# Keeping attention values unsplit in DRAM and splitting the first key block inside the head-pair loop

## What is computed

```
x = x + 0.5 * ffn(layernorm(x))      # routed low-rank experts, top 16 of 64
x = x + attn(layernorm(x))
x = x + 0.5 * ffn(layernorm(x))

# attn: 32 heads, the key and value width is 128
q, k, v = split(hidden @ wq), split(hidden @ wkv)
scores  = q @ k^T * scale, causal mask
attn    = softmax(scores) @ v
return attn.reshape(B, S, 32 * 128) @ wo
```

## Time and profile before

| | |
|---|---|
| median of 3 runs | 1045.79 us (1045.55 to 1046.63) |
| the profiled execution's own time | 1047.01 us |
| its span, first to last instruction | 1045.2 us |
| mean granted TensorE clock | 0.995 |
| TensorE busy | 1031.7 us, 99% of the span |
| VectorE, ScalarE, GpSimd busy | 689.6, 555.1 and 532.5 us |
| moved by transfers | 168.17 MB |

### The profile page before, as it was taken

One profiled execution on the slowest core, in us unless ns is written; L12 is line 12 of the kernel. 1 busy time (PEld: TensorE's weight loads), 2 busy tenths in 40 slices (PEclk: granted clock), 3 DMA queues, 4 the chain that ended last, 5 costly groups with the idle time before them and its releaser, 6 DMA issues.

```text
span 1045.2 us, 18708 instructions
## 1 busy us (share of the span) xinstructions
PE 1031.7 (99%) x5588; PEld 892.5 (85%) x5588; DVE 689.6 (66%) x1815; ACT 555.1 (53%) x1480; POOL 532.5 (51%) x472
## 2 busy tenths in 40 slices
PE   8999999999999999999999999999989999999998
PEld 8999788888788888888888888888878888889997
DVE  6778852433467677777667767766777988766553
ACT  4112455554366676676676676676676555531110
POOL 5431378996268777778777778777410000010000
PEclk9999999999999999999999999999989999999999
DMA  9700254772634443453443443443577878840000
GB/s 373 306 0 1 81 211 174 277 265 91 231 92 134 161 139 114 147 161 132 155 143 114 148 161 130 151 150 121 161 258 279 313 251 280 289 161 11 20 20 31
DMA packets 83704, 168.17 MB, mean 161 GB/s; under 512 B 8528, under 2 KB 24912, under 8 KB 82640
## 3 DMA queue, kind: packets, MB, share of 16 engines
q1 hardware_dynamic: 83664, 167.68, 46.5%
HBM read 102.37 MB, written 63.44 MB: 159 GB/s over the span
## 4 chain that ended last, share of the span: by engine, by line
PE 96%; DVE 2%; ACT 1%; DMA 1%; issue 0%; POOL 0%; POOLq 0%; ACTq 0%
PE bank L274 28%; PE bank L276 28%; PE bank L275 28%; PE bank L540 4%; PE bank L558 3%; PE bank L529 3%; PE bank L330 1%; PE bank L282 1%; DMA o_raw<-keep_o 1%; PE bank L356 0%; PE bank L517 0%; DVE x L1039 0%; DMA x<-x_in 0%; DVE ow_lo L935 0%; DVE o_lo L935 0%
## 5 line engine op out<-in xcount | busy, mean ns | idle before, releaser
L1280 POOL TENSOR_SCALAR ve<-mv 128x1 f32<-128x1 f32 x24 | 6.3, 264 | 309.3 <-DVE mv L942 309.1
L652 ACT ACTIVATE bank<-bank,nmax 128x128 f32<-128x128 f32 (+1 forms) x256 | 105.7, 455 | 1.2 <-DVE nmax L1056 1.1
L1069 DVE TENSOR_SCALAR prob<-bank,rinv 128x128 f32<-128x128 f32 (+1 forms) x256 | 95.1, 413 | 4.6
L1056 DVE CUSTOM_DVE_ANT_0 bank<-bank,mask 128x128 f32<-128x128 f32 (+1 forms) x256 | 83.6, 389 | 18.7 <-PE bank L276 18.7
L274 PE MATMUL bank<-xc_lo,wq_hi 128*128 128x512 f32 x224 | 93.4, 417 | 1.0 <-ACT s7q L606 0.7
L274 PE MATMUL bank<-o_lo,ow_hi 128*128 128x512 f32 x224 | 89.7, 401 | 4.0 <-DVE o_lo L935 4.0
L276 PE MATMUL bank<-o_hi,ow_hi 128*128 128x512 f32 x224 | 88.4, 395 | 0.0
L275 PE MATMUL bank<-o_hi,ow_lo 128*128 128x512 f32 x224 | 88.2, 394 | 0.0
L274 PE MATMUL bank<-xc_lo,wk_hi 128*128 128x512 f32 x224 | 87.6, 391 | 0.3 <-ACT s L606 0.3
L276 PE MATMUL bank<-xc_hi,wq_hi 128*128 128x512 f32 x224 | 87.8, 392 | 0.0
L606 ACT CAST o_hi<-o_raw 128x1024 fp32r<-128x1024 f32 x56 | 59.2, 1057 | 53.4 <-DMA o_raw<-keep_o 44.6
(11 more groups left out here) (166 smaller groups left out, 3153.4 us busy)
## 6 DMA issues: line engine op xcount, KB each, us to landing
o_raw<-keep_o SPq DMA_DIRECT2D x49, 512.0 KB, 4.1
keep_v<-out_hl SPq DMA_DIRECT2D x64, 256.0 KB, 2.3
v<-keep_v SPq DMA_DIRECT2D x64, 256.0 KB, 3.5
keep_o<-att_comb SPq DMA_DIRECT2D x60, 256.0 KB, 2.6
keep_o<-att SPq DMA_DIRECT2D x45, 256.0 KB, 3.2
stage_v<-wv SPq DMA_DIRECT2D x4, 2048.0 KB, 9.1
stage_wq<-wqk SPq DMA_DIRECT2D x16, 512.0 KB, 3.3
keep_vraw<-out_raw SPq DMA_DIRECT2D x64, 128.0 KB, 2.1
```

The source lines that it names most:

```text
L652: nc.scalar.activation(sp[b][:, a:e], sp[b][:, a:e], ACT.Exp, bias=nmax[:, c:c + 1], scale=-1.0, accum_out=rsum[:, c:c + 1]).then_inc(s["e ...
L1056: nc.vector.tensor_tensor_reduce(out=sp[b][:, a:e], in0=sp[b][:, a:e], in1=mask[:, a:e], scale=-SCALE, scalar=BIG, op0=ALU.add, op1=ALU.mi ...
L1069: nc.vector.tensor_scalar(prob[:, b, a:e], sp[b][:, a:e], rinv[:, c:c + 1], None, ALU.mult).then_inc(s["p_ready"], 1)
```

## The change

For every tile of V the plain sum is stored, even c too. The tiles out_hl and out_raw become one tile out_v for each of two buffers, `keep_v` and `keep_vraw` become one tensor, and the 32 lo subtractions and 24 of the 32 roundings of the V phase go (the other eight become plain copies of block 3). In the pair loop `load_v` puts the plain first key block where lo will stand (v_in is the same memory as v). ACT rounds it into the hi part (`act_v_split`), and DVE subtracts in place (`dve_v_split`), one instruction each for both sequences of a half, 128 partitions by 2x256 elements. Half 1 of pair p is split in stage 1 of pair p, half 0 of pair p + 1 in stage 3 of pair p, half 0 of pair 0 in the prologue: 32 instructions on each engine. TensorE now waits for the semaphore v_split where it waited for v0_loaded and v1_loaded. The core of the diff:

```diff
-                if c % 2 == 0:
-                    pe.wait_ge(s["v_low"], low_count(g - 1, 3, c))
-                else:
-                    pe.wait_ge(s["v_raw12"], 2 * (g - 1) + c // 2 + 1)
+                pe.wait_ge(s["v_raw12"], TH * (g - 1) + c + 1)
...
             if j == 0:
-                pe.wait_ge(s["v0_loaded"], 64 * p + 64)
+                pe.wait_ge(s["v_split"], 2 * p + 1)
             elif j == 2:
-                pe.wait_ge(s["v1_loaded"], 64 * p + 64)
+                pe.wait_ge(s["v_split"], 2 * p + 2)
...
         def act_v_last_block(act, g):
-            act_v_high(act, g, 3, 0)
-            act_v_plain(act, g, 1)
-            act_v_high(act, g, 3, 2)
-            act_v_plain(act, g, 3)
+            for c in range(TH):
+                act_v_plain(act, g, c)
+
+
+        def act_v_split(act, p, half):
+            act.wait_ge(s[f"v{half}_loaded"], 64 * p + 64)
+            act_copy(v[:, half, :, 0, :], v_in[:, half, :, 1, :]).then_inc(s["v_hi_done"], 1)
...
                 act_attended(act, p, j)
+                if j == 1:
+                    act_v_split(act, p, 1)
+                elif j == 3 and not final:
+                    act_v_split(act, p + 1, 0)
...
-        def dve_v_low(dve, g, block, c):
-            dve.wait_ge(s["v_hi_done"], low_count(g, block, c))
-            lo(out_high(block, c, 1), v_src(block, c), out_high(block, c, 0)).then_inc(s["v_low"], 1)
+            wait_stored(dve, g, block, c)
+            nc.vector.tensor_tensor(out_plain(block, c), a, b, ALU.add).then_inc(s["v_sum"], 1)
+
+        def dve_v_split(dve, p, half):
+            dve.wait_ge(s["v_hi_done"], 2 * p + half + 1)
+            lo(v[:, half, :, 1, :], v_in[:, half, :, 1, :], v[:, half, :, 0, :]).then_inc(s["v_split"], 1)
...
                 if j < 2 or not final:
                     dve_softmax_max(dve, u + 2, j)
+                if j == 1:
+                    dve_v_split(dve, p, 1)
+                elif j == 3 and not final:
+                    dve_v_split(dve, p + 1, 0)
...
-                sp_.dma_start(v[:, half, b, :, :].rearrange("p l n -> p (l n)").bitcast(F32),
-                              keep_v[bass.ds(p, 1), half, b, :, :].rearrange("o p n -> (o p) n")).then_inc(s[f"v{half}_loaded"], 16)
+                sp_.dma_start(v_in[:, half, b, 1, :],
+                              keep_v[bass.ds(p, 1), half, 2 * b, :, :].rearrange("o p n -> (o p) n")).then_inc(s[f"v{half}_loaded"], 16)
```

More of the change, by code:

```diff
@@ L174, in build_macaron @@
         vs17 = place("vs17", [P, TH, D], F32, at=where["s1"])
[L175 to L180, removed]
+        out_v = [place("out_v0", [P, TH, 2, 2 * DH], F32, at=at + 32 * D),
+                 place("out_v1", [P, TH, 2, 2 * DH], F32, at=where["v"])]
+        v_in = place("v_in", [P, 2, 2, 2, 2 * DH], F32, at=where["v"])
+        keep_v = nc.dram_tensor("keep_v", [PAIRS, 2, TH, P, 2 * DH], F32, kind="Internal").ap()
         half1_raw = place("half1_raw", [P, 2, 2, HALF], F32, at=where["xc_lo"] + 4 * 2 * HALF * B12)
@@ L420, in v_count @@
             return 3 * TH * g + TH * (1, 3, 4).index(i) + c + 1
-        def low_count(g, block, c):
-            return 8 * g + 2 * block + c // 2 + 1
         def sum_count(g, block, c):
@@ L445, in pe_v @@
             elif i == 3:
[L446 to L449, removed]
+                pe.wait_ge(s["v_sum"], sum_count(g, 0, c))
             elif i == 4:
@@ L706, in act_c12 @@
             act_rounded(g, 3, acc[g][:, :])
-        def out_high(block, c, part):
-            return out_hl[block % 2][:, c // 2, :, part, :]
         def out_plain(block, c):
-            return out_raw[block % 2][:, c // 2, :, :]
-        def v_src(block, c):
-            return (vacc[c] if block == 3 else vyz[c])[:, :].rearrange("p (h n) -> p h n", h=2)
+            return out_v[block % 2][:, c, :, :]
         def wait_stored(eng, g, block, c):
@@ L747, in act_v_snap @@
             act_copy(dst[:, c, :], v_bank(i, c)[:, :]).then_inc(s[name], 1)
[L749 to L756, removed]
         def act_v_plain(act, g, c):
@@ L1108, in dve_v_sum @@
             b = (vs2 if block == 1 else vs17)[:, c, :].rearrange("p (h n) -> p h n", h=2)
[L1109 to L1114, removed]
-        def dve_v_low(dve, g, block, c):
-            dve.wait_ge(s["v_hi_done"], low_count(g, block, c))
-            lo(out_high(block, c, 1), v_src(block, c), out_high(block, c, 0)).then_inc(s["v_low"], 1)
-        def dve_v_block(dve, g, block):
[L1121 to L1126, removed]
+            wait_stored(dve, g, block, c)
[3 more added lines that the diff above has]
+            lo(v[:, half, :, 1, :], v_in[:, half, :, 1, :], v[:, half, :, 0, :]).then_inc(s["v_split"], 1)
+        def dve_v_block(dve, g, block):
+            for c in range(TH):
+                dve_v_sum(dve, g, block, c)
         def dve_v_group(dve, g):
@@ L1515, in load_v @@
             for b in range(2):
-                sp_.dma_start(v[:, half, b, :, :].rearrange("p l n -> p (l n)").bitcast(F32),
-                              keep_v[bass.ds(p, 1), half, b, :, :].rearrange("o p n -> (o p) n")).then_inc(s[f"v{half}_loaded"], 16)
+                sp_.dma_start(v_in[:, half, b, 1, :],
+                              keep_v[bass.ds(p, 1), half, 2 * b, :, :].rearrange("o p n -> (o p) n")).then_inc(s[f"v{half}_loaded"], 16)
                 sp_.dma_start(v_raw[:, half, b, :],
-                              keep_vraw[bass.ds(p, 1), half, b, :, :].rearrange("o p n -> (o p) n")).then_inc(s[f"v{half}_loaded"], 16)
+                              keep_v[bass.ds(p, 1), half, 2 * b + 1, :, :].rearrange("o p n -> (o p) n")).then_inc(s[f"v{half}_loaded"], 16)
         def load_stage_v(sp_, g):
@@ L1528, in store_v @@
             for c in range(TH):
-                if c % 2 == 0:
-                    sp_.wait_ge(s["v_low"], low_count(g, block, c))
-                elif block < 3:
+                if block < 3:
                     sp_.wait_ge(s["v_sum"], sum_count(g, block, c))
                 else:
-                    sp_.wait_ge(s["v_raw12"], 2 * g + c // 2 + 1)
+                    sp_.wait_ge(s["v_raw12"], TH * g + c + 1)
                 for h in range(2):
                     pair = 4 * g + 2 * row + h
-                    if c % 2 == 0:
-                        dst, src = keep_v[pair, half, c // 2], out_hl[block % 2][:, c // 2, h, :, :].rearrange("p l n -> p (l n)").bitcast(F32)
-                    else:
-                        dst, src = keep_vraw[pair, half, c // 2], out_raw[block % 2][:, c // 2, h, :]
-                    sp_.dma_start(dst, src).then_inc(s[f"stored{block % 2}_{c}"], 16)
+                    sp_.dma_start(keep_v[pair, half, c], out_v[block % 2][:, c, h, :]).then_inc(s[f"stored{block % 2}_{c}"], 16)
         def load_w(sp_, g, p):
@@ L1761, in _ @@
                         pe_v(pe, g, i, c)
-            pe.wait_ge(s["v_low"], low_count(GROUPS - 1, 2, 2))
+            pe.wait_ge(s["v_sum"], 12 * GROUPS)
             pe_m1(pe, "q", 0)
@@ L1883, in _ @@
             act_c12(act, "k", 0)
+            act_v_split(act, 0, 0)
             act_pair(act, 0, first=True)
@@ L1999, in _ @@
             dve_c12(dve, "k", 0)
+            dve_v_split(dve, 0, 0)
             dve_pair(dve, 0, first=True)
```

24 lines of the change are left out of this document (4 added, 20 removed).

## The result

The changed kernel took 1050.08 us, median of 5 runs (1048.85 to 1051.19), against 1045.79 (1044.96 to 1046.82) of the kernel before: ratio 1.0033, 95% interval 1.0023 to 1.0044. Predicted were 1049.2 us, between 1046.6 and 1051.7, with "slower" as the likeliest sign. Run again beside more runs of the kernel before (experiment e0), the ratio was 1.0028 (1.0018 to 1.0038).

A forecast was written before the change was run, and what follows sets the result against it. The kernel was taken as bound by TensorE's own work, so relief elsewhere counts 0; added waits of 1.7 + 0.95 + 0.2 + 0.6 = 3.45 us took the median from 1045.79 to 1049.2 us, range 1046.6 to 1051.7.

The forecast's parts named there:

- slower: Sign of the whole change: slower 0.72, the same 0.25, faster 0.03; 2.1 us taken as the least difference measurable.
- The V phase: V phase: removing 32 DVE subtractions (22 us) and 24 ACT roundings gains 0, since TensorE did not wait there.
- The hold-up by POOL: Beside POOL: DVE's subtraction with both operands in SBUF stands until POOL's instruction is over and ends 0.55 us after it.
- Rival B: POOL's cast does not hold DVE's subtraction up: about 1.0 us in all, 1046.8; with a cheaper queue step, together 0.23.
- Rival C: Pair ends: POOL's subtraction goes first and DVE waits; 3.7 us per pair, 52 us in 14, 1099 us; chance 0.06.
- Rival D: Stage 0's wait is passed on to POOL and ACT: another 0.3 us per pair, 4 us, 1053; chance 0.08.
- Stage 3 to stage 0: Ends of pairs 0 to 13: late pT_lo makes TensorE's matmul 0.12 us late per pair, 1.7 us in 14.
- Prologue: Prologue, once: DVE's subtraction waits for POOL's cast, so the load behind pT_lo comes 0.95 us later.
- before the last pair: Before the last pair, once: the subtraction waits for POOL's attention block, so ow_lo starts 0.2 us later.
- last pair: Stage 1 of the last pair, once: TensorE's load for m = 4 waits for o_lo, the full 0.6 us.
- Stage 1: Stage 1, 15 times: the subtraction needs 0.60 us, DVE idles 0.47 there; TensorE has slack, so cost 0.
- The clock (rival E): Low-clock stretch after the wait before the last pair shortens or lengthens; gone altogether with rival B, 1044.4; chance 0.03.

The follow-up runs named there:

- e0: The changed kernel run again without edit, beside the kernel before: 1049.78 us against 1046.93, ratio 1.0028.
- e3: Changed kernel with the splits at pair ends and in the prologue moved to idle time, the last pair's subtraction behind o_lo: 1046.42 us, ratio 0.9997 to the kernel before.
- e6: Kernel of e3 with DVE's 48 sums and ACT's 16 plain copies of the V phase done twice: 1047.04 us, ratio 0.9996 to the kernel before.
- e2: Changed kernel with DVE's subtraction at each pair's end put behind kT_lo instead of ahead of it: 1111.81 us, ratio 1.062 to the kernel before.
- e1: Changed kernel with half 0's split moved to idle time (ACT's rounding to stage 2's end, DVE's subtraction behind stage 3's pT_lo): 1048.03 us, ratio 1.0009 to kernel before.

## Why the prediction was right

**The V phase: right.** 0 was taken. e3, which keeps the relief and none of the added waits, is no faster than the kernel before, and e6 puts back more of DVE's work than was removed without a trace of it in the time.

**The hold-up by POOL: right.** That DVE's subtraction would stand until POOL's cast was over, and end 0.55 us after it, was worked out from an instruction half as long beside another operation of POOL. It ended 0.54 after. Its duration was 0.86 us, not the 0.78 forecast: it starts with the softmax's last instruction, where kT_lo had started 0.08 behind it, and so 0.32 us before the cast's end in place of 0.23. The end is set by POOL, so pT_lo was 0.7 us late as forecast. Rival B fell at the trace. Rival C was a real danger, 0.3 us away: e2 made its hold-up happen, behind kT_lo and not ahead of it, and it costs 65 us, more than the 53 of rival C, because the clock came on top. Rival D is out: TensorE lost 1.04 us in the 14 places, and the 14 pairs as a whole grew by no more.

**Stage 3 to stage 0: mechanism right, 1.0 us in place of 1.7.** The load came 0.22 us after pT_lo's end, near the 0.25 taken. The mis-sized piece is the step from load to matmul: 0.10 was carried over from stage 3, and the matmul started 0.04 after its load (581.07, 581.11), at its usual pace of 0.23 us behind the one ahead. What was lost was the next one's pace, 0.18 us to the second matmul in place of 0.11. So 0.07 per pair, not 0.12. The prediction had named a cheaper step there as a part of rival B, but as all or nothing.

**Prologue, before the last pair, last pair: 0.95, 0.2 and 0.6 forecast; 0.87, 0.18 and 0.60 measured.** In the prologue the load followed pT_lo by 0.05 us (297.37 to 297.42) and not by 0.13. e3 takes all three and the pairs' 1.0 away, and the time returns to that of the kernel before. In all, 3.45 us were forecast and 2.7 stand in the trace; 4.3 between the first medians and 2.9 in e0 lie on either side of the forecast, so that 1049.2 came so near the first median is in part luck.

**Stage 1: right.** The subtraction takes 0.68 us there (0.6 forecast) and the 15 places show no wait.

**The clock (rival E)** went the kind way, by 0.85 us in the profiled executions. The execution from which the forecast started had lost some 0.9 us more to the low clock ahead of the last pair than the others that have a trace, and it stood 1.2 us above the median; that the one explains the other is not shown (15 of the 31 runs of the kernel before show a mean clock of 0.995 or less, as it did). To add the sum to the median, and not to that execution, was the safe choice.

## What to carry to other kernels

Ahead of placing an instruction on DVE beside a busy POOL, look at where its operands are and at what POOL has begun at that moment: the same 128x512 subtraction took 0.69 us with an operand in PSUM or POOL idle, 0.86 and 1.93 behind a cast, and 3.72 behind a long subtraction that had started 0.3 us before. Then read the slack of the tile that waits behind it: here half a microsecond was free and all beyond it was paid, so one subtraction cost 0.07 us a pair (0.05 with its operand in PSUM) and two of the latter cost 0.92. Relief on an engine that nobody waits for is no counterweight; moving the new work into a gap of the same engine cost nothing that can be measured and took the whole loss back.

## What the runs showed of the hardware beyond that

- A copy from SBUF to SBUF on DVE (fp32 in, fp32r out) is held up by POOL's cast as well, although it has a single operand: 0.42 us alone, 0.60 and 1.68 beside casts, each time ending 0.28 us after them. With the subtraction it is 0.55. That is what is left of the instruction once POOL is through, and it differs by as much as the two take alone (0.69 - 0.42 = 0.27).
- The holding goes both ways: POOL's subtraction of 3.50 us took 3.82 behind DVE's, its cast of 0.40 took 0.89.
- Waits of 3 us every 34 us left the clock alone for four pairs and then brought it down for part of each pair, which added 1.3 to 2.9 us to a pair. The one wait of nearly 4 us ahead of the last pair brought it down 2.5 us after TensorE's last matmul in the kernel before, 4.1 us after in the changed one and 5.0 in e1.
